# First image pair of a state-space scan: input terms in PSUM, states summed by TensorE

## The reference, cut to what matters

```python
def step(h, inp):
    dt_t, B_t, C_t, x_t = inp
    dA = jnp.exp(dt_t[..., None] * A)
    dBx = dt_t[..., None] * B_t[:, None, :] * x_t[..., None]
    h = dA * h + dBx
    y = jnp.einsum('bdn,bn->bd', h, C_t)
    return (h, y)
...
dt = jax.nn.softplus(dt_low @ W_dt + b_dt)
y = _selective_scan(xh, dt, Bmat, Cmat, A, D)
y = y * jax.nn.silu(z)
return y @ W_out
```

## Time and profile before

| | us |
|---|---|
| median of three runs (2176.43 to 2183.86) | 2176.59 |
| the profiled execution's own time | 2186.44 |
| its span, first to last instruction | 2184.6 |
| busy PE / DVE / POOL / ACT | 1713.5 / 1372.9 / 1016.5 / 651.0 |

### The profile page before, as it was taken

How to read it: one execution, slowest core, us unless ns; L and a number is a source line. 1 busy time by engine, 2 the same in 40 slices (tenths; PEclk the granted TensorE clock), 3 DMA queues, 4 the chain that set the end, 5 groups by cost and what they waited for, 6 DMA issues and landing times.

```text
span 2184.6 us, 17479 instructions
## 1 busy us (share of the span) xinstructions
PE 1713.5 (78%) x6245; PEld 983.5 (45%) x6245; DVE 1372.9 (63%) x1516; ACT 651.0 (30%) x983; POOL 1016.5 (47%) x708
## 2 busy tenths in 40 slices
PE   2024354347999987999999979999998899999885
PEld 1011121014564543665555635655465466664552
DVE  3497799954467996648899956568997300124224
ACT  1003133112424333333344333423532322222210
POOL 1788855877752347775643477863343000000000
PEclk7556565568999997899999979999999799999557
DMA  8453202023531132343311332432121012210000
GB/s 167 110 140 95 63 20 70 24 75 104 132 101 35 44 82 64 88 116 87 97 46 52 81 95 86 114 95 77 29 58 44 0 44 63 54 44 10 1 0 10
DMA packets 174926, 148.43 MB, mean 68 GB/s; under 512 B 137972, under 2 KB 138360, under 8 KB 174840
## 3 DMA queue, kind: packets, MB, share of 16 engines
q1 hardware_dynamic: 147192, 71.78, 13.7%
q0 software_dynamic: 27648, 75.53, 12.2%
HBM read 132.01 MB, written 15.24 MB: 67 GB/s over the span
## 4 chain that ended last, share of the span: by engine, by line
PE 54%; DVE 23%; issue 5%; ACT 4%; DMA 1%; POOL 0%; DVEq 0%; SPq 0%; ACTq 0%; POOLq 0%
PE ps L801 39%; PE ps L804 10%; DVE tiles L1387 4%; DVE tiles L1380 4%; DVE tiles L1395 3%; DVE slot L1334 2%; PE ps L1016 2%; DVE slot L1338 1%; PE ps L846 1%; DMA mring<-mixing 1%; ACT tiles L619 1%; DVE sampled L1345 1%; ACT tiles L716 1%; ACT tiles L621 1%; DVE normal L1278 1%
## 5 line engine op out<-in xcount | busy, mean ns | idle before, releaser
L565 POOL DMA_INDIRECT slot<-corners,index x576 | 723.1, 1255 | 271.3 <-issue 163.3
L801 PE MATMUL ps<-toep,tiles 128*128 128x512 f32 (+3 forms) x2048 | 589.6, 436 | 4.2 <-DMA mring<-mixing 1.9
L801 PEld LDWEIGHTS ps<-toep,tiles 128*128 128x128 f32 x2048 | 368.8, 191 | 232.1 <-issue 134.0
L581 POOL TENSOR_TENSOR tiles<-tiles 128x1024 f32<-128x1024 f32 x120 | 291.3, 2427 | 355.9 <-DVE tiles L1387 343.0
L1387 DVE TENSOR_TENSOR_SCAN tiles<-tiles 128x1024 f32<-128x1024 f32 x128 | 301.2, 2353 | 12.3
L700 ACT COPY tiles<-ps 128x512 f32<-128x512 f32 x256 | 149.6, 585 | 466.3 <-PE ps L801 466.0
L801 PE MATMUL ps<-tiles,sel 96*128 96x512 bf16 x512 | 162.7, 442 | 137.6 <-DVE tiles L1395 116.1
L804 PE MATMUL ps<-tiles,mring 128*128 128x128 f32 (+2 forms) x1024 | 243.8, 381 | 0.0
L801 PE MATMUL ps<-tiles 128*128 128x64 f32 (+5 forms) x770 | 197.1, 401 | 36.1 <-ACT tiles L716 17.6
L685 ACT ACTIVATE tiles<-tiles,negA 128x1024 f32<-128x1024 f32 x128 | 146.8, 1149 | 233.6 <-DVE tiles L1387 212.7
L804 PEld LDWEIGHTS ps<-tiles,mring 128*128 128x128 f32 x1024 | 167.2, 191 | 77.5 <-issue 66.0
(11 more groups left out here) (231 smaller groups left out, 1772.6 us busy)
## 6 DMA issues: line engine op xcount, KB each, us to landing
toep<-in_phi_pad_dram SPq DMA_DIRECT2D x64, 513.0 KB, 4.0
mring<-mixing SPq DMA_DIRECT2D x128, 128.0 KB, 4.4
slot<-corners,index POOLq DMA_INDIRECT x576
corners<-turned SPq DMA_DIRECT2D x128, 64.0 KB, 1.9
corners<-tiles SPq DMA_DIRECT2D x4, 648.0 KB, 4.9
residual<-in_x_dram SPq DMA_DIRECT2D x4, 512.0 KB, 3.9
mixing<-tiles SPq DMA_DIRECT2D x8, 256.0 KB, 4.5
out_dram<-residual SPq DMA_DIRECT2D x4, 512.0 KB, 2.7
```

What stands on the lines that cost most here:

```text
L565: g.indirect_dma_start(out=slots[number % 3][:, k, :, :].rearrange("p a c -> p (a c)"), out_offset=None, in_=tables[h], in_offset=bass.Ind ...
L581: g.tensor_tensor(f(Y[h]), f(Y[h]), f(HC[n % 2]), ALU.add).then_inc(*ysum.up())
L801: return t.matmul(o, w, r, start=start, stop=stop)
```

## The change

It has four parts.

1. **Input terms in place, pair 0 only.** `input` writes its product over the B rows in ps2, and `scan` reads its second operand from ps2. So `b rows` of the next state waits for the scan, not for `input`, and DVE's order becomes input, scan, product instead of scan, next input, product.
2. **States summed by PE, pair 0 only.** POOL's 32 `sum` units are gone. Instead PE has a unit `sum`: two float32 matmuls of 128x512 with the identity as weights, which add the product (now always in one of the two HC tiles) into `sums` (ps0, two PSUM banks). Each stands behind the next state's `b rows` and `c rows`. `product` waits for PE's sum two states back, and `finish y` reads the sum from ps0.
3. **Heads in halves, all pairs.** `x in` waits for its own half of the image only; `exp ln` and `step sizes` are split into halves of 512 tokens, with a signal for each.
4. **Turns anew.** The whole of `TURNS` is replaced, for all pairs.

```diff
@@ class Plan @@
-            act += both("silu x") + both("silu z") + both("copy rows") + both("soft") + [("exp ln", j, h)]
-            dve += both("split rows") + [("step sizes", j, h)]
+            act += both("silu x") + both("silu z") + both("copy rows")
+            for q in (2 * h, 2 * h + 1):
+                act += [("soft", j, q), ("exp ln", j, q)]
+            dve += both("split rows") + both("step sizes")
...
+                if j == 0:
+
+                    pe += [("b rows", j, s), ("c rows", j, s)] + ([("sum", j, s - 1)] if s % N_STATE else [])
+                    dve += [("scan", j, s), ("product", j, s)]
...
 TURNS = {
     "POOL": """
-        A122 B A3 B A3 B A4 B A4 B A4 B A4 B10 A4 B A3 B A B A B A B A B A B A B A B A B A B A B A B A B A2 B A122 B32 A123 B
...
+        A263 B A2 B A6 B A6 B A6 B A B A B A3 B25 A127 B A4 B A B A B A3 B A4 B A4 B26 A144 B32""",
...
@@ pe @@
-                pe.wait_ge(*x1_ok.at(j, 2 * h + 2))
+                pe.wait_ge(*x1_ok.at(j, 2 * h + q + 1))
...
-                if some(bin_ok.at(j, s)):
-                    pe.wait_ge(*bin_ok.at(j, s))
+
+                read = scan_ok if in_place(j) or s == 0 else bin_ok
+                if some(read.at(j, s)):
+                    pe.wait_ge(*read.at(j, s))
...
+            def sum_states(j, s):
+                h, n = s // N_STATE, s % N_STATE
+                pe.wait_ge(*hc_ok.at(j, s + 1))
+                if n == 0 and h == 1:
+                    pe.wait_ge(*y2_ok.at(j, 1))
+                for q in range(2):
+                    last = t.matmul(sums[:, HALF * q:HALF * q + HALF], ident, F[:, HC[n % 2], HALF * q:HALF * q + HALF],
+                                    start=n == 0, stop=n == N_STATE - 1, skip_group_check=True)
+                last.then_inc(*first_sum.up())
@@ dve @@
-                v.tensor_tensor(f(DBX[s % 2]), f(DTX[s // N_STATE]), ps[2][:], ALU.mult).then_inc(*bin_ok.up())
+                to = ps[2][:] if in_place(j) else f(DBX[s % 2])
+                v.tensor_tensor(to, f(DTX[s // N_STATE]), ps[2][:], ALU.mult).then_inc(*bin_ok.up())
...
-                v.tensor_tensor_scan(f(HS), f(DA[s % 2]), f(DBX[s % 2]), 0.0, ALU.mult, ALU.add).then_inc(*scan_ok.up())
+                given = ps[2][:] if in_place(j) else f(DBX[s % 2])
+                v.tensor_tensor_scan(f(HS), f(DA[s % 2]), given, 0.0, ALU.mult, ALU.add).then_inc(*scan_ok.up())
```

More of the change, by code:

```diff
@@ L163, in scan @@
             for s in range(N_STATE * h, N_STATE * h + N_STATE):
-                pe += [("b rows", j, s), ("c rows", j, s)]
                 act += [("decay", j, s)]
-                pool += [("sum", j, s)]
                 if s % N_STATE == 0:
                     dve += [("input", j, s)]
+                if j == 0:
+                    pe += [("b rows", j, s), ("c rows", j, s)] + ([("sum", j, s - 1)] if s % N_STATE else [])
+                    dve += [("scan", j, s), ("product", j, s)]
+                    if s % N_STATE == N_STATE - 1:
+                        pe += [("sum", j, s)]
+                    else:
+                        dve += [("input", j, s + 1)]
+                    if s == N_STATE:
+                        dve += [("finish y", j, 0)]
+                    continue
+                pe += [("b rows", j, s), ("c rows", j, s)]
+                pool += [("sum", j, s)]
                 dve += [("scan", j, s)]
@@ L748, in work @@
                 if unit == "exp ln":
-                    exp_ln_head(j, m)
+                    exp_ln_head(j, m // 2, m % 2)
                 if unit == "decay":
@@ L1106, in work @@
                     c_rows(j, m)
+                if unit == "sum":
+                    sum_states(j, m)
                 if unit == "out":
@@ L1392, in product @@
                 dve.wait_ge(*c_ps.at(j, s + 1))
-                if some(ysum.at(j, s - 1)):
-                    dve.wait_ge(*ysum.at(j, s - 1))
-                v.tensor_tensor(f(Y[h]) if n == 0 else f(HC[n % 2]), f(HS), ps[3][:], ALU.mult).then_inc(*hc_ok.up())
+                if some(summed(j, s - 1)):
+                    dve.wait_ge(*summed(j, s - 1))
+                to = f(Y[h]) if n == 0 and not in_place(j) else f(HC[n % 2])
+                v.tensor_tensor(to, f(HS), ps[3][:], ALU.mult).then_inc(*hc_ok.up())
             def finish_y(j, h):
-                dve.wait_ge(*ysum.at(j, N_STATE * (h + 1)))
-                link(v.scalar_tensor_tensor(out=f(Y[h]), in0=f(XC[h]), scalar=dskip, in1=f(Y[h]), op0=ALU.mult, op1=ALU.add))
+                dve.wait_ge(*summed(j, N_STATE * (h + 1)))
+                link(v.scalar_tensor_tensor(out=f(Y[h]), in0=f(XC[h]), scalar=dskip, in1=sums[:] if in_place(j) else f(Y[h]),
+                                            op0=ALU.mult, op1=ALU.add))
                 v.tensor_tensor(f(Y[h]), f(Y[h]), f(SZ[h]), ALU.mult).then_inc(*y2_ok.up())
```

115 lines of the change are left out of this document (62 added, 53 removed).

## The result

The changed kernel takes 2126.26 us (median of four runs, 2124.78 to 2131.55) where the kernel before takes 2180.23 on the same chip: a ratio of 0.9757, 95% interval 0.9728 to 0.9786. The forecast was 2151.6 and faster; the direction is right, and the gain of 54 us is about twice the 25 that were forecast. The profiled execution took 2131.55 us, its span is 2129.7.

A forecast was written before the change was run, and what follows sets the result against it. PE's 471 idle microseconds could be won, with DVE bounding pair 0's scans and PE the stretch to `taps`. 2186.4 - 21 (`out` of pair 1) - 4 (later pairs) = 2161.4; 9.8 lower for the median, 2151.6; 8-in-10 range 2122 to 2179.

The forecast's parts named there:

- the hole: PE nearly idle between `taps` of pair 0 and `out` of pair 1: its 28 us were to be gone.
- The PSUM operand: Pair 0's `input` writing to PSUM and scan reading there: priced at nothing, upper bound 79 us for 32 scans.
- The waits of DVE before `out` of pair 0: Five counted waits in DVE's stretch, together 28 us, put `out` of pair 0 at 461.5, 9 us later than before.
- `add conv`: In DVE's stretch, DVE waits three times for PE's five matmuls: 12 us.
- head of the second image: Wait of DVE at the second image's head before `out` of pair 0: 6 us.
- 17 us from `taps` to `out` of pair 1: `evict` and layer norm after `taps` of pair 0, timed from the next pair: 17 us, `out` of pair 1 at 816.5.
- The chain of norms: From `out` of pair 0 to `begin`: 65 us with head matmuls and `conv samples` in its gaps, against 61.4 before.
- the stretch to `taps`: From `begin` to `taps` of pair 0: 294.9 less 17 of work and 5 of idle time, 273 us.
- The later pairs: Gain of 4 us after `out` of pair 1, from a little more filler in the chain after `out`.
- Heads in halves for pairs 1 to 3: Lie beside PE's work: nothing; if DVE were the bound there, 1.3 us per pair.
- The gain eaten by waits: Rival: PE stays at the lower level through pair 0's scans, 2178 us, about as before; chance 0.14.
- More than forecast: Rival: 15 of the 28 us of waits fall away, chains of pairs 1 and 2 better filled, 2131 us; chance 0.13.

The follow-up runs named there:

- e1: Changed kernel with POOL again summing the states of pair 0, all else kept: 2179.66 us against 2183.92 of the kernel before, ratio 0.9982.
- e2: Kernel before with only PE's sums and input terms in PSUM for pair 0, heads whole, old turns: 2173.56 us, ratio 0.9942 to the kernel before.
- e3: Changed kernel with input terms of pair 0 in two SBUF buffers again instead of PSUM: ratio 0.9767 to the kernel before.
- e5: The changed kernel measured again, unaltered, in another session: ratio 0.9742 to the kernel before.
- e4: Changed kernel with whole heads (exponential, logarithm, step sizes once for 1024 tokens) in all pairs: 2148.0 us, ratio 0.9827 to the kernel before.
- e12: Changed kernel with whole heads in pairs 1 to 3 alone, halves in pair 0: 2138.46 us, ratio 0.9797 to the kernel before.
- e9: Kernel before with PE's sums, input terms in PSUM and heads in halves, but the old turns: 2168.2 us, ratio 0.9917 to the kernel before.
- e6: Changed kernel with PE's sums cut to one matmul of 128 columns for 28 of pair 0's 32 states: 2130.27 us, ratio 0.9753 to the kernel before.
- e7: Changed kernel with PE adding every state of pair 0 twice, four matmuls of 512 columns per state: ratio 0.9820 to the kernel before.
- e8: Changed kernel with input terms of pair 0 in SBUF again, a repeat run: 2131.28 us, ratio 0.9765 to the kernel before.

## Why the prediction was right, and where its size was off

**The direction and the mechanism.** Of the signs it named, these are in the profile: scans of pair 0 at 2.3 us (2286 ns), 238 us of DVE work from start to start (254.1 less 16.2 of waits) where 239.9 was summed, a clock above 0.7 (0.79), no POOL sum before pair 1, the last scan of pair 1 (to 760.6) ahead of the end of `taps` (778.2), and 17.5 of the 28 us of the hole gone, with a rest of 10.9 that is `evict` and the layer norm. Two are not: `out` of pair 0 came at 446.1 and not near 461, `taps` at 778.2 and not near 800. e1 and e2 show that the mechanism is right as well: more groups of pair 1 ahead shorten PE's stretch and close the hole (e1 has both), and only with POOL's sums out are they to be had without losing as much before (e2 beside e1). The PSUM operand, priced at nothing between bounds up to 79 us, costs nothing (e3). That it also keeps scans and POOL out of each other's way was in the prediction for fetches alone, and not for the scans beside sums.

**The size.** The forecast span was 2159.6, the measured one 2129.7. In the median the miss is 25.3 us, since the forecast took the profiled execution to lie 9.8 above the median, and it lay 5.3 above. The 30 us are four terms; a fifth point does not show in the sum:

- *The waits of DVE before `out` of pair 0: 28 summed (its five terms add up to 28.5), 16.2 measured*, 12 of the 30. Term by term: `add conv` 12 against 10.1, head of the second image 6 against 0.8, first fetches of pair 1 2.5 against 0.3, last sum 3 against 2.1, PE late with rows 5 against 2.4; 0.5 more is a scan that waited for its `input`. The head was the largest error: the 6 us had no row behind them, and in this stretch of the kernel before DVE waited 2.0 us for it. With 1.6 for the start and 2 for the work, `out` of pair 0 came 15.4 earlier than forecast, and earlier than before, where the prediction had set "9 us **later** than before". These steps and the start are together 15.4 of the 30.
- *17 us from `taps` to `out` of pair 1: 10.9 measured*, 6 of the 30. The step that failed is "in the next pair, where nothing was late, took from 1250.7 + 5.6 to 1273.3". Something was late there. The timeline of the kernel before, between the two rows:

```profile
1261.29 3.78 PE L801 MATMUL ps<-residual,cst 128*128 128x512 f32 x4 [4.99 <-DVE residual L1533]
1267.54 3.39 PE L801 MATMUL ps<-tiles,cst 128*128 128x512 f32 x4 [2.47 <-ACT tiles L615]
```

  PE stood idle for 4.99 us, since `evict` was queued on DVE behind positions and the two operations of `finish y` of pair 2, and the norm's matmuls after it took 3.78 and 3.39 us, all or most of that at the lower level. With `evict` prompt (1.77) and the level kept they take 1.99 and 1.98, and the way is 10.6 to 10.9. The level is not sure even then: in e5, the same kernel, `evict` was as prompt (1.79) and the two steps took 3.68 and 2.94, and the way from `taps` to `out` of pair 2 was 13.2.
- *The chain of norms, 65 against 61.8, and the stretch to `taps`, 273 against 270.3*: 6 of the 30. The filler in the chain's gaps cost it nothing (61.4 before). In the stretch PE's work fell by the 17 us that were forecast (279.8 to 262.9), and its idle time by 7.7 instead of 5.
- *The later pairs, 4 against 6.6*: 2.6. They won by the gap above, 6.4 at `out` of pair 2, and not by the filler in the chains that the prediction gave as the reason: the number is near, the reason was another.
- *Heads in halves for pairs 1 to 3: nothing* in the sum. e4 and e12 put 7 to 17 us on them in the new turns, e9 with e2 5 in the old ones. This did not show in the sum as an error of its own, because the stretch from `out` of pair 1 to the next `taps` came out as long as before (420.3 against 418.9) instead of longer. What in those turns needs the halves was not isolated; what the whole heads cost there shows as a lower clock.

**The rivals.** "The gain eaten by waits" rested on PE at the lower level all through. With its sums PE reached 0.79, so the case did not come, and no run has the full sums at the lower level to price it: e6 ran at 0.61 without loss, but with the sums cut, and e7 shows how near the edge is with them doubled. "More than forecast" was the case that came, 5 us beyond its 2131, and by its first reason in the main: 12 of its 15 us of waits fell away, though not at `add conv` (10.1 of 12). Its second, better filled chains, did not come (61.8 us against 61.4), and the late `evict` was in no rival. The time came within 5 us of the lower end of the range, 2122 to 2179. The gap behind the late `evict`, 6 us here and 6.4 one pair on, was not reckoned with in it, and that it did not carry the time out of the range is luck.

## What to carry to other kernels

Work moved off a shared queue pays only when the order of everything behind it is made anew: here PE's sums and the input in place gave 10 to 12 us in the old order, everything but PE's sums 4, and all together 54. Before a row is taken as "the time of this step when nothing is late", read what ended the idle time inside it; the 17 us were a late `evict` and the lower clock behind it. And a write in place that makes one engine wait for another's last read was free in pair 0, where the waiting engine has room, and cost some 57 us in pairs 1 to 3, where that engine is the bound.

## What the runs showed of the hardware

- A scan of 128x1024 takes the same with its second operand in PSUM (2286 ns) as in SBUF (2291 ns), where POOL has no sums beside it.
- With both operands in SBUF a scan holds up POOL's indirect fetches: all 50 fetches that began during such a scan in e3 and e8 ended 0.75 to 0.76 us after it. With one operand in PSUM it does not: 44 of 45 took 0.94 to 0.95 us. In the mean of the stretch that is 1418 and 1422 ns for a fetch against 1113.
- The same holds against POOL's sums: with both operands in SBUF six scans of the kernel before that met a sum took 2.93 to 2.94 us instead of 2.29; with one operand in PSUM (e1) no scan took more than 2.29, though six had a sum beside them for over 2.1 us.
- Thirty-four microseconds of extra PE work in DVE's stretch raised the granted clock from 0.61 to 0.79 and left the end where it was (e6 against the changed kernel).
- After a longer gap on PE the lower level followed, after a short one mostly not. At the two matmuls of the norm ahead of `out` of pair 2, a gap of 4.09 to 5.01 us was followed by 3.78 us in all four profiles that have one (the kernel before, e2, e4, e9). A gap of 1.58 to 1.79 us was followed by 1.98 or 1.99 us in nine of ten, and by 3.68 in e5, after 1.79.
